# An attention and expert kernel: index products with the code columns stationary, sums turned in two parts

## The reference

```python
h = layernorm(x) * (1 + ca) + sa
q, k, v = split(h @ qkv_w.T + qkv_b)                 # 16 heads of 8 features
score = sigmoid(sigmoid(relu(h @ r_w1.T + r_b1) @ r_w2.T + r_b2))
keep = top_k(score, 819) per head                    # int(2048 * 0.4) keys
w = softmax(q @ k.T / sqrt(8)) over the kept keys
x = x + ga * (w @ v)
h = layernorm(x) * (1 + cb) + sb
e = argmax(softmax(h @ router_w.T))                  # one of 8 experts per token
x = x + gb * (relu(h @ fc[e]) ** 2 @ proj[e].T)
```

## Time and profile before

| | us |
|---|---|
| median of 3 runs | 651.76 (650.35 to 652.49) |
| the profiled execution | 651.93 |
| its span, first to last instruction | 650.1 |
| PE busy | 478.0 |
| DVE busy | 397.3 |
| ACT busy | 307.8 |
| POOL busy | 204.6 |

### The profile page before, as it was taken

How to read it: one execution, slowest core, us unless ns; L and a number is a source line. 1 busy time by engine, 2 the same in 40 slices (tenths; PEclk the granted TensorE clock), 3 DMA queues, 4 the chain that set the end, 5 groups by cost and what they waited for, 6 DMA issues and landing times.

```text
span 650.1 us, 9970 instructions
## 1 busy us (share of the span) xinstructions
PE 478.0 (74%) x3510; PEld 240.4 (37%) x3510; DVE 397.3 (61%) x1051; ACT 307.8 (47%) x431; POOL 204.6 (31%) x282
## 2 busy tenths in 40 slices
PE   4763524877999789869979969968999987006994
PEld 4322424722333233323323313323333336005994
DVE  8789501386787548738747747846888665301562
ACT  4342000004776447727736736736776584004662
POOL 4000575035100540460270171072000200450886
PEclk9786555555897859959959978987999795557998
DMA  7528600000000000000000000000000002022231
GB/s 231 92 96 240 168 7 4 2 2 7 1 12 16 5 3 27 4 5 27 3 6 26 2 6 27 2 7 11 16 4 1 2 2 66 24 75 63 24 30 13
DMA packets 26348, 22.06 MB, mean 34 GB/s; under 512 B 6272, under 2 KB 22464, under 8 KB 26304
## 3 DMA queue, kind: packets, MB, share of 16 engines
q1 hardware_dynamic: 15632, 16.55, 8.9%
q0 software_dynamic: 7296, 2.96, 4.0%
q10 hardware_dynamic: 3376, 1.98, 1.7%
HBM read 12.88 MB, written 8.93 MB: 34 GB/s over the span
## 4 chain that ended last, share of the span: by engine, by line
PE 55%; DVE 19%; issue 14%; POOL 6%; DMA 2%; ACT 2%; another core or an unknown queue 1%; POOLq 0%; SPq 0%; DVEq 0%; ACTq 0%
PE OP L1369 15%; PE ST L1353 9%; DVE tile_max L981 8%; PE SC L1310 5%; PE ST L1334 5%; PE SC L1277 5%; PE SC L1312 4%; POOL out L616 4%; DVE B L914 2%; PE OP L1377 2%; POOL slots_dram L608 2%; DVE PR L839 1%; DMA KV<-slots_dram 1%; PE ST L1329 1%; PE OP L1442 1%
## 5 line engine op out<-in xcount | busy, mean ns | idle before, releaser
L981 DVE TENSOR_REDUCE tile_max<-SC 128x1 f32<-128x410 f32 (+1 forms) x512 | 272.0, 577 | 116.6 <-PE SC L1310 54.9
L699 ACT ACTIVATE PR<-ST 128x1024 f32<-128x1024 f32 (+1 forms) x224 | 206.8, 962 | 93.6 <-PE ST L1353 70.0
L522 POOL DMA_INDIRECT G<-kv_dram,idx x104 | 106.1, 1020 | 87.8 <-DVE idx L930 53.1
L1353 PE MATMUL ST<-QS,KT 51*128 51x512 bf16 (+1 forms) x416 | 121.5, 423 | 11.1 <-issue 7.0
L1369 PE MATMUL OP<-PR,VS 128*32 128x512 f32 x768 | 116.9, 685 | 0.6 <-ACT PR L699 0.6
L1310 PE MATMUL SC<-KT,QS 48*128 48x410 bf16 x256 | 80.8, 382 | 8.4 <-issue 5.6
L1353 PEld LDWEIGHTS ST<-QS,KT 51*128 51x128 bf16 (+1 forms) x416 | 36.5, 100 | 99.7 <-issue 82.5
L1312 PE MATMUL SC<-KT,QS 48*128 48x409 bf16 x128 | 48.8, 381 | 24.8 <-issue 12.3
L1277 PE MATMUL SC<-B,ABUF 128*64 128x7 f16 x512 | 35.3, 259 | 38.7 <-issue 23.8
L1277 PEld LDWEIGHTS SC<-B,ABUF 128*64 128x64 f16 x512 | 34.2, 215 | 40.2 <-issue 40.2
L616 POOL DMA_INDIRECT out<-PR,owner x24 | 37.7, 1569 | 28.5 <-issue 27.5
(11 more groups left out here) (234 smaller groups left out, 597.4 us busy)
## 6 DMA issues: line engine op xcount, KB each, us to landing
kv_dram<-KV SPq DMA_DIRECT2D x4, 512.0 KB, 2.9
WE<-in_w_fc SPq DMA_DIRECT2D x1, 2048.0 KB
WE<-in_w_proj SPq DMA_DIRECT2D x1, 2048.0 KB
G<-kv_dram,idx POOLq DMA_INDIRECT x104
slots_dram<-zeros ACTq DMA_DIRECT2D x1, 1548.0 KB, 11.4
KV<-slots_dram SPq DMA_DIRECT2D x1, 1548.0 KB, 7.8
q_parts_dram<-QP SPq DMA_DIRECT2D x3, 512.0 KB, 3.8
QS<-q_parts_dram SPq DMA_DIRECT2D x16, 96.0 KB
```

The source lines that it names most:

```text
L522: pool.indirect_dma_start(G[:, i % 2, slot_of(s), :], None, kv_dram, bass.IndirectOffsetOnAxis(ap=idx[:, i, s:s + 1].bitcast(U32), axis=0) ...
L699: nc.scalar.activation(PR[:, k, 0:cols], ST[:, (KSTEPS * n + k) % 2, 0:cols], ACT.Exp, scale=float(D) ** -0.5).then_inc(exp_done, 1)
L981: v.tensor_reduce(tile_max[:, n % 2, at_col:at_col + 1], bank(RING_AT["unit", u])[:, 0:410 - f], AX.X, ALU.max).then_inc(s_reduced, 1)
L1353: last = mm(ST[:, at_step % 2, 512 * e:512 * e + 512], KT[rows, i % 2, P * tile:P * tile + P], QS[rows, i % 2, CHUNK * c:CHUNK * (c + 1)], ...
```

## The change

Five edits; in words, and then the core of the diff.

- `index_mm`: the 14 code columns of a tile are stationary and the 64 one-hot columns move. One product for a tile and head instead of two, 32 for a pair. The result has codes as rows (0 to 13 for head 0, 32 to 45 for head 1), in `OP` and `ST` or `SC` by turns.
- ACT copies these rows to `by_code` (two copies for a pair), and a new `row_to_partition(i)` on PE brings them by two fp32 products to the 128 x 13 form that `index(i)` reads.
- The code columns come from `columns(h0, h1)`: two plain products over 2, 2 and 12 heads (compare, then times token), with `onehot(1)` and `index(0)` ahead of the large one. The intermediate table lies in the space of `WE`, so SP loads the experts' weights only after all tables are done, behind `m_rows(0)`.
- In the main loop `turn_o` comes in two parts of two products, with a unit between, and `turn_m` behind both. One unit moves from behind the first `weigh` to behind the second; `weigh_shared` stands behind step 5 instead of step 6. Score halves take whichever head the next unit does not.
- `TURN_AFTER` goes from 8 to 7, which is bookkeeping for the bank that `turn_k` takes.

```diff
-            for n, w_part in enumerate((w_fc, w_proj)):
-                sp.dma_start(WE[:, :, HD * n:HD * (n + 1)], w_part.rearrange("n p c -> p n c"))\
-                    .then_inc(we_in, 16)
...
             m_rows(0)
+            sp.wait_ge(idx_ready, NP)
+            for n, w_part in enumerate((w_fc, w_proj)):
+                sp.dma_start(WE[:, :, HD * n:HD * (n + 1)], w_part.rearrange("n p c -> p n c"))\
+                    .then_inc(we_in, 16)
             for n in range(NCH):
...
+            for i in range(NP):
+                act.wait_ge(idx_mm, i + 1)
+                if i >= 2:
+                    act.wait_ge(row_mm, i - 1)
+                for e in range(2):
+                    rows = slice(32 * e, 32 * e + CODES)
+                    nc.scalar.activation(by_code[rows, i % 2, :], tokens_of(i)[0][rows, :], ACT.Copy)\
+                        .then_inc(code_copied, 1)
...
-            def codes_rest():
-                for col in range(CODES):
-                    number = 2 * (col % BLOCKS) + col // BLOCKS
-                    last = v.scalar_tensor_tensor(B1[:, 2:H, :, col], key_of[:, 2:H, :], float(number),
-                                                  token.rearrange("p (h t) -> p h t", h=1).to_broadcast([P, H - 2, NT]),
-                                                  ALU.is_equal, ALU.mult)
-                last.then_inc(codes_ready, 1)
+            def columns(h0, h1, step):
+
+                n = h1 - h0
+                v.tensor_tensor(B0[:, h0:h1, :, :], key_of[:, h0:h1, :].rearrange("p h (t a) -> p h t a", a=1)
+                                .to_broadcast([P, n, NT, CODES]),
+                                cc("code").rearrange("p (h t c) -> p h t c", h=1, t=1).to_broadcast([P, n, NT, CODES]),
+                                ALU.is_equal).then_inc(column_step, 1)
+                dve.wait_ge(column_step, step)
+                v.tensor_tensor(B1[:, h0:h1, :, :], B0[:, h0:h1, :, :],
+                                token.rearrange("p (h t c) -> p h t c", h=1, c=1).to_broadcast([P, n, NT, CODES]),
+                                ALU.mult).then_inc(columns_ready, 1)
...
+                pe.wait_ge(columns_ready, min(i + 1, 3))
                 pe.wait_ge(onehot_ready, 2 * i + 2)
                 if i >= 2:
-                    pe.wait_ge(idx_ready, i - 1)
+                    pe.wait_ge(code_copied, 2 * (i - 1))
                 for e in range(2):
                     for t in range(NT):
-                        for hi in range(2):
-                            last = mm(SC[HALF * hi:HALF * (hi + 1), [0, 2][i % 2], 6 * e:6 * e + BLOCKS],
-                                      A1[:, i % 2, e, :, t], B1[:, 2 * i + e, t, BLOCKS * hi:BLOCKS * (hi + 1)],
-                                      start=(e == 0 and t == 0), stop=(e == 1 and t == NT - 1), skip_group_check=True)
+                        last = mm(tokens_of(i)[0][32 * e:32 * e + CODES, :], B1[:, 2 * i + e, t, :], A1[:, i % 2, e, :, t],
+                                  start=(t == 0), stop=(t == NT - 1), skip_group_check=True)
                 last.then_inc(idx_mm, 1)
 
+            def row_to_partition(i):
+
+                pe.wait_ge(code_copied, 2 * i + 2)
+                if i >= 2:
+                    pe.wait_ge(idx_ready, i - 1)
+                to_row = cc("to_row").rearrange("p (w s) -> p w s", w=2)
+                for hi in range(2):
+                    last = mm(tokens_of(i)[1][HALF * hi:HALF * (hi + 1), :], by_code[:, i % 2, :], to_row[0:64, hi, :],
+                              start=True, stop=True)
+                last.then_inc(row_mm, 1)
...
                 for k in range(KSTEPS):
-                    scores(n, k, 0)
-                    unit()
+
+                    e = 1 - ORDER[units[0]][3] if units else 0
                     if k == 3:
+                        scores(n, k, 0, True)
+                        unit()
+                        if n >= 1:
+                            turn_o(n - 1, (0, 1))
+                        unit()
+                        if n >= 1:
+                            turn_o(n - 1, (2, 3))
                         if n + 1 < NCH:
                             turn_m(n + 1)
-                        if n >= 1:
-                            turn_o(n - 1)
-                    else:
-                        scores(n, k, 1)
+                        continue
+                    scores(n, k, e, True)
+                    unit()
+                    scores(n, k, 1 - e, False)
                     unit()
                     if k == 1:
                         if n >= 1:
                             weigh(n - 1, (5, 6))
                         unit()
-                        unit()
                     if k == 2 and n % NQ == 1 and n // NQ + 1 < NP:
                         turn_k(n // NQ + 1)
                     if k == 4:
                         weigh(n, (0, 1), first=True)
-                weigh_shared(n)
+                        unit()
+                    if k == 5:
+                        weigh_shared(n)
                 weigh(n, (2, 4))
```

More of the change, by code:

```diff
@@ L109, in constants @@
     cols["token"] = (CT * js + P * u)[None, :] + p[:, None]
[L110 to L111 removed]
+    cols["code"] = np.broadcast_to(np.arange(CODES), (P, CODES))
+    to_row = np.zeros((P, 2, STEPS))
+    for e in range(2):
+        for c in range(CODES):
+            to_row[32 * e + c, c % 2, 6 * e + c // 2] = 1
+    cols["to_row"] = to_row.reshape(P, -1)
     add = np.zeros((P, NP, STEPS))
@@ L934, in _ @@
             dve.wait_ge(place_ready, 1)
-            codes_first()
+            columns(0, 2, 1)
             onehot(0)
-            codes_rest()
+            columns(2, 4, 2)
+            onehot(1)
             index(0)
-            for i in range(1, NP):
+            columns(4, H, 3)
+            for i in range(2, NP):
                 onehot(i)
-                if i >= 2:
-                    index(i - 1)
+                index(i - 1)
             index(NP - 1)
@@ L1329, in turn_m, with turn_o, scores @@
                 nc.tensor.transpose(turned_m(n), NMB[:, 1::2], identb[:, :]).then_inc(mtr_done, 1)
-            def turn_o(n):
+            def turn_o(n, tiles):
                 pe.wait_ge(o_copied, n + 1)
-                for t in range(4):
+                for t in tiles:
                     last = mm(turned_o(n)[:, 32 * t:32 * t + 32], OS[:, P * t:P * t + P], cc("sum_groups"),
                               start=True, stop=True)
-                last.then_inc(otr_done, 1)
-            def scores(n, k, e):
+                if tiles[-1] == 3:
+                    last.then_inc(otr_done, 1)
+            def scores(n, k, e, first):
                 i, c = n // NQ, n % NQ
                 at_step = KSTEPS * n + k
-                if e == 0:
+                if first:
                     if at_step >= 2:
@@ L1354, in scores @@
                           QS[rows, i % 2, CHUNK * c:CHUNK * (c + 1)], start=True, stop=True)
-                if e == 1 or k == 3:
+                if not first or k == 3:
                     last.then_inc(st_filled, 1)
@@ L1433, in _ @@
                         weigh(n, (0, 1), first=True)
-                weigh_shared(n)
+                        unit()
+                    if k == 5:
+                        weigh_shared(n)
                 weigh(n, (2, 4))
+                unit()
+                assert not units
             weigh(NCH - 1, (5, 6))
-            turn_o(NCH - 1)
+            turn_o(NCH - 1, (0, 1, 2, 3))
             def route(g):
```

52 lines of the change are left out of this document (25 added, 27 removed).

## The result

The changed kernel took 627.55 us (median of 4 runs, 624.26 to 630.77) and the kernel before, beside it, 651.52 (650.35 to 652.49). The ratio is 0.9633, with a 95% interval of 0.9569 to 0.9696. The ratios leave out executions more than 1.5% above the fastest of the same kernel, so they can differ a little from the quotient of two medians. The direction and the range of 600 to 637 were right, but the forecast of 616.5 promised 11 us too much, and its own range of 607 to 627 was just missed. The profiled executions took 629.86 and 651.93, spans 628.1 and 650.1, and I account for these 22.1 us.

The account below looks back on a forecast made before the run. It took slow instruction supply to PE under gathers to bound the index stage, and DVE's gaps to cost the loop time. 651.9 - 20.2 (stage) + 1.0 (weights' load) - 16.2 (loop) = 616.5 us; own range 607 to 627, 8-in-10 range 600 to 637.

Parts of the forecast that it names:

- Table 0 and the price of a product: Index stage: removing L914 brings table 0 at 59.6 instead of 69.5, with products at 0.07 us each.
- The stage's end: Index stage: last table at 105.7 instead of 125.9, two pairs of heads left at 3.5 us each; 20.2 us gained.
- By the supply above: Index stage under gathers: instructions reach PE at 2.1 products per us, so 38.1 us bring 80 of 252 instruction pairs.
- rival 2: Index stage: fewer instructions don't shorten the stall, only table 0's 9.9 us are won; 626.8 us, chance 0.12.
- The loop, undisturbed: Main loop: closing DVE's gaps takes an undisturbed chunk from 10.0 to 9.25 us; 15 intervals give 11.3 us.
- PE (7 to 8 us from start to start without waits): Main loop: PE's work in an undisturbed chunk, claimed to fit in the forecast 9.25 us.
- The loop, with gathers: Main loop: stalls stay, but the rest of chunks with gathers gains 0.83 us in each of six windows, 5.0 us.
- The weights' load: Chunks 0 and 1: the experts' weights load later, ahead of chunk 1's rows of maxima; 1 us charged, ends 0 and 10.
- 1 (the loop keeps its pace): Main loop: PE, ACT and `ST` hold each chunk, DVE's gap only moves; 632.7 us, chance 0.18.
- 3 (the stop hardly bites): Index stage under gathers: PE's pauses let supply fill up, gain 30 there, some 18 in the loop; 604 us, chance 0.10.
- 4 (rows of maxima bound the loop): Main loop: rows of maxima come late at 31 chunk borders; slower, 663.7 us at 1.0 us a chunk, chance 0.06.

Follow-up runs that it names:

- e2: Kernel before with only the changed main loop, old index stage kept: 547.98 us, ratio 0.9459.
- e3: Changed kernel with the intermediate code table in another buffer, so the experts' weights load where the kernel before had it: 547.4 us, ratio 0.9415.
- e9: Repeat of e2's kernel (old index stage, changed loop) on a third chip: 551.13 us, ratio 0.9549.
- e8: Changed kernel with pair 1's gathers waiting until all index tables are done: 618.92 us, ratio 0.9568.
- e5: Kernel before, unedited, profiled again on the second chip of the experiments: 655.2 us, one run.
- e6: Changed kernel, unedited, run again on the same chip as e5: 628.66 us, ratio 0.9666.
- e10: Changed kernel with one gather instead of 13 for pairs 2 to 7: 551.85 us, ratio 0.9546.
- e11: Changed index stage with the loop of before, one gather instead of 13 for pairs 2 to 7: 586.97 us, ratio 1.0113.
- e12: Changed kernel with both e3's early weights' load and e8's later gathers of pair 1: 545.33 us, ratio 0.9432.
- e1: Changed kernel with the main loop of before, so the index stage's change alone: 585.1 us beside 580.2 for the kernel before.

## Why the prediction was right or wrong

**Table 0 and the price of a product.** Forecast 59.6, first gather 60.6; measured 60.70 and 61.88. The step was mis-sized by its product: 0.1075 us, inside its bounds of 0.063 and 0.142 and near their middle, not at the end I chose. The round for a pair of heads came to 4.30 us, not 3.5, and so is longer than the 3.84 before. The new form has half the products, and each takes nearly twice as long. Its gain is the serial work it takes away (L914) and not PE time. Where nothing stops, that leaves 4.2 us of stage (e2 and e3).

**The stage's end.** Forecast 105.7, 20.2 us gained; measured 112.34, 13.5. The step that failed is "By the supply above", the 2.1 products per us that brought 80 instruction pairs in the stall: I took the stop for a shortage of instructions that a leaner stream buys off, so that two pairs of heads would be left. The end of the stop was foreseen (98.7, measured 98.43). More than three pairs were left, each 0.8 us dearer: of the 6.7 us, 1.6 are the price of two pairs and 5.1 the work that was left over. The runs put late hand-overs in its place: the 15.6 us of the stop, in which that supply would have brought some 33 pairs, went by between the end of PE's products and one copy on ACT, no piece of instructions was loaded in them, and the same 448 products took 27 us on a chip without stops (e2, e9). e8 removed the long stop by moving gathers, not instructions. That comes near to rival 2's mechanism, though the number of instructions left behind the stop did fall. Rival 2's time of 626.8 came close to the 627.55, but not by its own terms: it had 9.9 from the stage and 16.2 from the loop, and the measured parts are 13.5 and 8.8. The Trainium skill ("Runtime: NRT & Kernel Launch", Instruction fetch mechanics) calls the crossing of a block "mostly hidden"; the piece that lay at hand through the stop of the kernel before (72.9 to 107.6) and e2's unbroken 27.07 us agree with that, and I had weighed it too low.

**The loop, undisturbed.** Forecast 9.25 a chunk, measured 9.48. The gap at the turning did go from 0.62 to at most 0.37, but three gaps of 0.24 to 0.37 stay, each before a bank from L1338. PE's 9.37 of 9.48 suggests why there was no more to have: PE looks like the bound of this chunk now, where the prediction had "PE (7 to 8 us from start to start without waits)" fit in. Still the 19 intervals without gathers gave 13.2 us where I had 11.3 for 15 and nothing for four. That was luck: only 6.7 came from the chunk (12 x 0.49 and 6 x 0.13), and 6.5 from the clock, which was low there for 20.5 us before and for 4.1 after. The term had no clock in it.

**The loop, with gathers.** Forecast 5.0 gained in six windows; measured 2.8 lost in five. This is the largest error, 7.8 us. I let the part of such a chunk outside the stop gain as elsewhere. PE's idle time in the window stayed (7.3 and 7.6 us; 35.0 and 34.6 over the five), while the time at half clock in the five windows went from 75.1 us to 84.6: what the denser loop won, the clock took back. The loss repeats in e5 and e6 (154.7 and 157.8 us, of which 75.1 and 81.7 at half clock). e10 and e11 don't show it, as they have no stop. That the longer time at half clock is due to the denser work is argued, not shown.

**The weights' load.** Forecast 1 us, measured 1.6 for chunks 0 and 1 together (13.4 against 11.8 in chunk 1), and 0.8 in the repeat (e5, e6). The forecast's reason is not seen in it: no wait of PE in chunk 1 ends with rows of maxima, and no run there took the load away. On chips without the stop chunk 1 is 3.8 us longer with the late load (15.5 in e10, 11.7 in e3, another batch), and there PE does wait for the rows queued behind the load:

```profile
129.96 0.61 PE L1384 MATMUL ST<-QS,KT 51*128 51x512 bf16 x1 [0.60 <-DMA QS<-MT]
```

But that is 0.60 us. The rest is PE busy for 14.92 us instead of 11.27, at a granted clock of 0.58 instead of 0.85; what kept the clock low is open.

**The sum.** Stage 6.7 less than forecast, windows 7.8 less, load 0.6 more, undisturbed chunks 1.9 better, 0.35 behind the loop: 13.5, against 35.4 - 22.1 = 13.3; the rest is rounding.

**The rivals.** 1 (the loop keeps its pace) is false for the undisturbed chunk, which went from 10.0 to 9.48; the loop's 8.8 net are 13.2 won and 4.4 lost. 3 (the stop hardly bites) is false on the first chip. On two others nothing stops at all, with either index stage (e2, e3), so its gain of 30 in the stage isn't there either. 4 (rows of maxima bound the loop) is false: 9.48 us a chunk on every chip. The wait for them at chunk 0, 1.61 us, was there before too (1.75).

**What stays open.** What in the chip makes hand-overs and PE's crumbs late while POOL gathers, no run here shows. Nor does one show why it happened in two batches and not in the two others: which chip the first batch ran on is not on record, and no kernel was run on one chip at two times. The changed kernel itself was not run on a chip without stops; e3, e10 and e12 stand in for it.

## What to carry to other kernels

When engines stand still while the one they wait for has long finished, and no load of instructions is under way, don't price it as a supply that a leaner stream stretches: find what runs beside it and move that, which here one wait on POOL did. Carry a new matrix product through the sum at both of its bounds unless a row has both its stationary and its moving width; the 0.07 taken here was a third too low. And a gain within a chunk at full clock carries over to a chunk with a stop in it only if the clock behind the stop does, so count those windows apart.

## What the runs showed of the hardware

The kernel before took 651.5 and 648.5 us in two batches and 580.2 and 585.0 in two others on other chips, with the same program. In the slower two, beside trains of indirect gathers (one every 1.31 us), PE runs in crumbs and a hand-over between engines can come 15.6 us late instead of 0.04; in the others not.

The loop's edit was worth 5.5 us where there are stops and 26 to 34 where there are none (e9 and e2 against the kernel before, e3 against e1, e10 against e11). Of the 34.1 us between e11 and e10, 20.5 went with the granted clock: the loop with PE busy 9.37 us of 9.48 was at 1.2 GHz for 17 us of 309, the one with 9.22 of 9.97 for 78 us of 343, in each case behind its first stretch.

14 stationary and 64 moving columns of fp16 took 0.1075 us, 64 stationary and 7 moving 0.061, both at 1.2 GHz.
